# Weight blocks of a dequantised feed-forward layer: one row of scales and one of zero points each, a fourth staging slot, and another order on VectorE and GpSimd

## The reference, cut to what matters

```python
def dequant_gptq(qweight, scales, zeros, groupsize):       # groupsize 128
    q = qweight[k // PACK, :] >> (k % PACK * 4)[:, None] & 15
    z = zeros[:, n // PACK] >> (n % PACK * 4)[None, :] & 15
    zp = (z.astype(jnp.float32) + 1.0) * s
    return q.astype(jnp.float32) * s[g] - zp[g]            # g = k // groupsize
gate = x2 @ Wg                                             # Wg, Wu: 512 x 1376
up = x2 @ Wu
inter = gate * jax.nn.sigmoid(gate) * up
out = (inter @ Wd).astype(jnp.float16)                     # Wd: 1376 x 512
```

## Time and profile before

| | |
|---|---|
| median of 3 runs | 893.2 us (892.1 to 893.83) |
| profiled execution, device time | 893.42 us |
| its span in the trace | 891.5 us |
| VectorE busy | 715.8 us |
| TensorE busy | 701.6 us |
| GpSimd busy | 542.7 us |
| ScalarE busy | 420.6 us |
| DMA engines busy, mean | 32% |

### The profile page before, as it was taken

How to read it: one execution, slowest core, us unless ns; L and a number is a source line. 1 busy time by engine, 2 the same in 40 slices (tenths; PEclk the granted TensorE clock), 3 DMA queues, 4 the chain that set the end, 5 groups by cost and what they waited for, 6 DMA issues and landing times. The chain is left out here.

```text
span 891.5 us, 8190 instructions
## 1 busy us (share of the span) xinstructions
PE 701.6 (79%) x2700; PEld 316.2 (35%) x2700; DVE 715.8 (80%) x719; ACT 420.6 (47%) x699; POOL 542.7 (61%) x281
## 2 busy tenths in 40 slices
PE   6986669998766978346643499798999978999895
PEld 3322123332211322011110144343445534787774
DVE  4846999989999999999999896988464573676657
ACT  2344776687646764555544224333334343522331
POOL 0008899989989999899999555577002031341152
PEclk9998868999878999567775599899999989999998
DMA  9102423331425432673322067983300020000011
GB/s 277 45 26 102 149 76 100 119 118 56 180 97 183 148 117 84 183 207 118 118 89 77 18 144 193 251 200 79 142 0 1 1 96 0 1 1 1 1 47 48
DMA packets 65212, 86.72 MB, mean 97 GB/s; under 512 B 18308, under 2 KB 32407, under 8 KB 64914
## 3 DMA queue, kind: packets, MB, share of 16 engines
q1 hardware_dynamic: 65170, 86.20, 32.0%
HBM read 74.97 MB, written 11.21 MB: 97 GB/s over the span
## 5 line engine op out<-in xcount | busy, mean ns | idle before, releaser
L1965 POOL TENSOR_TENSOR dbu<-rep_du,bc 128x1024 f32<-128x1024 f32 x128 | 299.0, 2358 | 6.4 <-DVE psum L1066 3.7
L1645 ACT ACTIVATE psum<-rep_dt,aneg 128x512 f32<-128x512 f32 x256 | 166.1, 682 | 148.2 <-DVE hc L1077 118.9
L1066 DVE TENSOR_TENSOR_SCAN psum<-psum,dbu 128x1024 f32<-128x1024 f32 x87 | 198.7, 2284 | 7.7 <-ACT psum L1645 5.1
L845 PE MATMUL psum<-hc,stk 128*32 128x512 f32 x512 | 91.8, 798 | 75.9 <-POOL hc L1974 38.0
L1077 DVE TENSOR_TENSOR hc<-psum,bc 128x1024 f32<-128x1024 f32 x87 | 106.5, 1224 | 3.4 <-PE psum L845 0.4
L1974 POOL TENSOR_TENSOR hc<-hc,bc 128x1024 f32<-128x1024 f32 x41 | 96.5, 2354 | 11.6 <-DVE hc L1066 11.4
L1066 DVE TENSOR_TENSOR_SCAN hc<-psum,dbu 128x1024 f32<-128x1024 f32 x41 | 93.5, 2280 | 6.6 <-ACT psum L1645 4.2
L642 PE MATMUL psum<-xf_hi,gu_hi 128*128 128x512 f16 x176 | 67.7, 385 | 0.0
L642 PE MATMUL psum<-xf_hi,gu_lo 128*128 128x512 f16 x176 | 67.4, 383 | 0.0
L642 PE MATMUL psum<-xf_lo,gu_hi 128*128 128x512 f16 x176 | 67.2, 382 | 0.0
L642 PE MATMUL psum<-xT,w_g 128*128 128x512 f32 x120 | 59.4, 640 | 6.9 <-DVE dt_t L1085 6.9
(11 more groups left out here) (225 smaller groups left out, 1399.1 us busy)
## 6 DMA issues: line engine op xcount, KB each, us to landing
rep_dt<-rep_scratch SPq DMA_DIRECT2D x60, 256.0 KB, 3.3
rep_du<-rep_scratch SPq DMA_DIRECT2D x60, 256.0 KB, 4.3
q_gu<-qgu_in SPq DMA_DIRECT2D x11, 512.0 KB, 4.5
z_gu<-zgu_scratch SPq DMA_DIRECT2D x11, 512.0 KB, 6.6
bc<-bc_scratch SPq DMA_DIRECT2D x16, 256.0 KB, 4.3
rep_scratch<-du_t SPq DMA_DIRECT2D x15, 256.0 KB, 2.0
rep_scratch<-dt_t SPq DMA_DIRECT2D x15, 256.0 KB, 2.3
q_d<-qd_in SPq DMA_DIRECT2D x11, 256.0 KB, 5.0
```

What stands on the lines that cost most here:

```text
L845: last = pe.matmul(y_rows(k), stk[:], hc[:, (i + k // 2) % HCS, k % 2, :], start=False, stop=(s == GN - 1))
L1066: dve.tensor_tensor_scan(h, a, dbu[:, i % DBS].rearrange("p e t -> p (e t)"), 0.0, ALU.mult, ALU.add)\
L1645: last = act.activation(psum[:, 2 * (i % 2) + e, :], rep_dt[:, cc % 2, k, :], ACT.Exp, scale=aneg[:, k, c, n:n + 1])
L1965: pool.tensor_tensor(dbu[:, i % DBS], rep_du[:, cc % 2, k:k + 2, :], bc[:, n, :].unsqueeze(1).broadcast_to([P, 2, L]), ALU.mult).then_inc( ...
```

## The change

The zero points and the scales of a block are stored near the start as one row each (1536 numbers: gate and up, then down), by four transfers instead of two. `stage(i)` loads each row by one transfer (`scl` and `zp`), so it issues four transfers. A fourth slot is added. It lies where the product's input of b = 1 lay, so `stage(3)` now waits for the last tile of `out_part`, and the loads for attention move behind the last use of that slot. GpSimd starts on gate and up as soon as their scaling is done, and makes `d_lo` of block i-1 after the zero points of block i. ScalarE waits for gate and up and for down apart; its order stays the same, but for one small copy of a gate weight that moves from k = 8 to k = 11. VectorE unpacks three blocks ahead, after the low half of the block before it, instead of four blocks ahead and before that low half.

```diff
-        STG = [155, 43, 171]
+        STG = [155, 43, 171, 125]
@@ stage(i), SyncE
-                s = i % 3
+                s = i % SLOTS
                 load(q_gu[s][:], ...)
                 load(q_d[s][:], ...)
-                load(s_gu[s][:]..., sgu_in[:, cols]...broadcast_to([P, 2 * KH, P]), ld_stage[s])
-                load(z_gu[s][:]..., zgu_dram[:, cols]...broadcast_to([P, 2 * KH, P]), ld_stage[s])
-                load(s_d[s][:], sd_in[i:i + 1, :].broadcast_to([P, H]), ld_stage[s])
-                load(z_d[s][:], zd_dram[i:i + 1, :].broadcast_to([P, H]), ld_stage[s])
+                load(scl[s][:], s_dram[i:i + 1, :].broadcast_to([P, SZ]), ld_stage[s])
+                load(zp[s][:], z_dram[i:i + 1, :].broadcast_to([P, SZ]), ld_stage[s])
@@ SyncE, order of the loads
-            stage_again(3)
-            for i in range(4, 7):
+            wait_taken(sp_, ("out", 1, NT - 1))
+            stage(3)
+            for i in range(SLOTS, IC):
                 stage_again(i)
-            wait_taken(sp_, ("out", 1, NT - 1))
+            sp_.wait_ge(wlo_gu, 8)
+            sp_.wait_ge(wlo_d, 8)
             load(wqraw[:].rearrange("p a b c -> p (a b c)"), wq_in, ld_att)
...
-            for i in range(7, IC):
-                stage_again(i)
@@ VectorE, feed-forward of b = 0
             unpack(0)
-            for i in range(1, 4):
+            for i in range(1, 3):
                 unpack(i)
                 low_weights(i - 1)
             for i in range(IC):
                 ffn_inner(0, i)
...
-                if i + 4 < IC:
-                    unpack(i + 4)
+                if i + 2 < IC:
+                    low_weights(i + 2)
                 if i + 3 < IC:
-                    low_weights(i + 3)
+                    unpack(i + 3)
-                if i == 7:
+                if i == 9:
                     dve.wait_ge(ld_att, 16 * 7)
@@ high_weights(i), ScalarE
-                act.wait_ge(w_done, 2 * (i + 1))
-                act.copy(gu_hi[:, i, :], w_gu[i % 3][:]).then_inc(whi_done, 1)
-                act.copy(d_hi[:, i, :], w_d[i % 3][:]).then_inc(whi_done, 1)
+                act.wait_ge(w_done, 2 * i + 1)
+                act.copy(gu_hi[:, i, :], w_gu[i % SLOTS][:]).then_inc(whi_done, 1)
+                act.wait_ge(w_done, 2 * i + 2)
+                act.copy(d_hi[:, i, :], w_d[i % SLOTS][:]).then_inc(whi_done, 1)
@@ GpSimd
             for i in range(IC):
-                s = i % 3
+                s = i % SLOTS
+                pool.wait_ge(q_done, 2 * i + 1)
+                pool.tensor_tensor(w_gu[s][:], w_gu[s][:], z_gu[s], ALU.subtract).then_inc(w_done, 1)
                 pool.wait_ge(q_done, 2 * i + 2)
-                pool.tensor_tensor(w_gu[s][:], w_gu[s][:], z_gu[s][:], ALU.subtract).then_inc(w_done, 1)
-                pool.tensor_tensor(w_d[s][:], w_d[s][:], z_d[s][:], ALU.subtract).then_inc(w_done, 1)
-                pool.wait_ge(whi_done, 2 * i + 2)
-                pool.tensor_tensor(d_lo[:, i, :], w_d[s][:], d_hi[:, i, :], ALU.subtract).then_inc(wlo_d, 1)
+                pool.tensor_tensor(w_d[s][:], w_d[s][:], z_d[s], ALU.subtract).then_inc(w_done, 1)
+                if i:
+                    low_down(i - 1)
+            low_down(IC - 1)
```

More of the change, by code:

```diff
@@ L41 @@
 NPAIR = NCH * QP
+SZ = 2 * KH * P + H
+SLOTS = 4
 BIG = 1e30
@@ L248, in build @@
         d_lo = at("d_lo", 114, [IC, H], F16)
-        STG = [155, 43, 171]
+        STG = [155, 43, 171, 125]
         q_gu = [at(f"q_gu{s}", k, [2 * KH * P], I32) for s, k in enumerate(STG)]
         w_gu = [at(f"w_gu{s}", k, [2 * KH * P]) for s, k in enumerate(STG)]
-        s_gu = [at(f"s_gu{s}", k + 4, [2 * KH * P], F16) for s, k in enumerate(STG)]
-        z_gu = [at(f"z_gu{s}", k + 6, [2 * KH * P]) for s, k in enumerate(STG)]
-        q_d = [at(f"q_d{s}", k + 10, [H], I32) for s, k in enumerate(STG)]
-        w_d = [at(f"w_d{s}", k + 10, [H]) for s, k in enumerate(STG)]
-        s_d = [at(f"s_d{s}", k + 12, [H], F16) for s, k in enumerate(STG)]
-        z_d = [at(f"z_d{s}", k + 13, [H]) for s, k in enumerate(STG)]
+        q_d = [at(f"q_d{s}", k + 4, [H], I32) for s, k in enumerate(STG)]
+        w_d = [at(f"w_d{s}", k + 4, [H]) for s, k in enumerate(STG)]
+        zp = [at(f"zp{s}", k + 6, [SZ]) for s, k in enumerate(STG)]
+        scl = [at(f"scl{s}", k + 12, [SZ], F16) for s, k in enumerate(STG)]
+        z_gu = [t[:, 0:2 * KH * P] for t in zp]
+        z_d = [t[:, 2 * KH * P:] for t in zp]
+        s_gu = [t[:, 0:2 * KH * P] for t in scl]
+        s_d = [t[:, 2 * KH * P:] for t in scl]
         xf_hi = [at(f"xf_hi{b}", k, [KH, L], F16) for b, k in enumerate([187, 195])]
@@ L329, in build @@
         rep_stored = sem("rep_stored")
-        ld_stage = [sem(f"ld_stage{s}") for s in range(3)]
+        ld_stage = [sem(f"ld_stage{s}") for s in range(SLOTS)]
         ld_att = sem("ld_att")
@@ L1231, in unpack @@
                                        ALU.bitwise_and))
-                dve.tensor_tensor(w_gu[s][:], q_gu[s][:], s_gu[s][:], ALU.mult).then_inc(q_done, 1)
-                dve.tensor_tensor(w_d[s][:], q_d[s][:], s_d[s][:], ALU.mult).then_inc(q_done, 1)
+                dve.tensor_tensor(w_gu[s][:], q_gu[s][:], s_gu[s], ALU.mult).then_inc(q_done, 1)
+                dve.tensor_tensor(w_d[s][:], q_d[s][:], s_d[s], ALU.mult).then_inc(q_done, 1)
             def low_weights(i):
                 dve.wait_ge(whi_done, 2 * i + 1)
-                dve.tensor_tensor(gu_lo[:, i, :], w_gu[i % 3][:], gu_hi[:, i, :], ALU.subtract).then_inc(wlo_gu, 1)
+                dve.tensor_tensor(gu_lo[:, i, :], w_gu[i % SLOTS][:], gu_hi[:, i, :], ALU.subtract)\
+                    .then_inc(wlo_gu, 1)
             def low_turned(b):
@@ L1857, in _ @@
                     high_weights(k + 3)
[L1858 removed]
+                if k == IC:
                     act.wait_ge(ld_att, 16 * 7)
@@ L1996, in _, with low_down @@
                         pool.tensor_tensor(x[:, t, :], x[:, t, :], obuf[0][:, t, :], ALU.add).then_inc(out_done, 1)
+            def low_down(i):
+                pool.wait_ge(whi_done, 2 * i + 2)
+                pool.tensor_tensor(d_lo[:, i, :], w_d[i % SLOTS][:], d_hi[:, i, :], ALU.subtract).then_inc(wlo_d, 1)
             for i in range(IC):
[L2000 removed]
+                s = i % SLOTS
+                pool.wait_ge(q_done, 2 * i + 1)
+                pool.tensor_tensor(w_gu[s][:], w_gu[s][:], z_gu[s], ALU.subtract).then_inc(w_done, 1)
                 pool.wait_ge(q_done, 2 * i + 2)
[L2002 to L2005 removed]
+                pool.tensor_tensor(w_d[s][:], w_d[s][:], z_d[s], ALU.subtract).then_inc(w_done, 1)
+                if i:
+                    low_down(i - 1)
+            low_down(IC - 1)
             def low_moe_weights(n, names):
```

31 lines of the change are left out of this document (13 added, 18 removed).

## The result

| | before | changed |
|---|---|---|
| median | 893.5 us of 4 runs (892.1 to 894.36) | 922.17 us of 4 runs (914.78 to 926.11) |
| ratio, 95% interval | | 1.031 (1.025 to 1.038) |
| profiled execution | 893.42 us, span 891.5 | 922.13 us, span 920.3 |
| `it(0)` | 547.72 | 551.58 |
| `it(0)` to `it(10)` | 88.6 us | 111.0 us |

The changed kernel is slower. Its two busiest elementwise engines are busy for less time than before, so it is not work that was added but waiting. Where it stands is seen in VectorE's rows in time over one iteration of the changed kernel (start, length, line, output and inputs, and in brackets the idle time before and what ended it). They answer to the earlier trace rows.

What follows compares the result with a forecast made beforehand. VectorE was taken to bound each feed-forward block at 8.79 us; the change's 10.9 us ring would delay `it(8)` by 22.0 us and the end by 22.2, 893.4 + 22.2 = 915.6, stated as 915.5 us, range 910 to 921.

Steps and rivals of the forecast that it cites:

- The ring: Feed-forward layer of b = 0: VectorE, GpSimd and ScalarE form one chain from `it(k)` to `it(k+1)`, 10.9 us per iteration against 8.8.
- the transfers are worth 0: Loads of weight rows: four issues for six, same bytes, no engine waiting from 542.3 us on; 0 us, slot 3 bound 0 to 2.
- VectorE is released by `sg`: Sign before each `it` of blocks 3 to 8: VectorE idle over 4 us until ScalarE's silu output `sg` releases it.
- the rest of the span is the same work in the same order, so a shift at `it` of block 10 is a shift of the end: After the feed-forward stage of b = 0: no weights unpacked, so its shift of 22.2 us carries unchanged to the end.
- which TensorE sets and which stays: Start of the feed-forward stage: `it(0)` stays at 547.72 us because TensorE's output product sets it.
- range: Whole kernel: 910 to 921 us, leaving out B, C and the ends of A and D.
- GpSimd's order: GpSimd in the feed-forward stage: no longer waiting for ScalarE between its three instructions gains nothing by itself, 51.7 of 94.0 us busy.
- A: TensorE's clock falls after each gap; next to nothing within the ring, 2.9 us once after `it(8)`: 918.4 us; chance 0.21.
- B: Feed-forward stage: the ring does not bind, TensorE sets 7.9 us per block, total 879 us; chance 0.06.
- C: Feed-forward stage: no change, a ring of about 8.8 to 9 us, early gains paying for later loss; chance 0.03.
- D: Load of slot 3 and its followers late, `unpack(3)` waiting up to 5 us once: 917 to 921 us; chance 0.08.
- VectorE loses 2.7 us a block to GpSimd before the change: Feed-forward blocks: `it_lo`, `q_gu` and `w_d` run long waiting for the shared SBUF port, about 2.7 us per block.

Runs made afterwards that it cites:

- the kernel with the ring opened: Changed kernel with ScalarE making the high halves of block k+2 in iteration k instead of k+3; 900.58 us against 895.8, ratio 1.006, iteration 8.79 us.

## Why the prediction was wrong in its number and right in its mechanism

**The ring** (the main step) was right. Term by term, from the rows above of the changed kernel and the earlier trace rows:

| term | forecast | measured |
|---|---|---|
| `it` to behind `it_lo` | 2.05 | 610.85 - 608.81 = 2.04 |
| `gu_lo` | 1.14 | 611.99 - 610.85 = 1.14 |
| `q_gu`, `q_d`, `w_gu` | 2.33 | 614.30 - 611.99 = 2.31 |
| `w_d`, then GpSimd's two | 0.69 + 3.5 = 4.19 | 618.45 - 614.30 = 4.15 |
| `d_hi`, silu, handovers | 1.2 | 619.60 - 618.45 = 1.15 |
| sum | 10.9 | 10.79 |

In the fourth term the way differed and the size did not: GpSimd starts 0.17 us after `w_d` begins, and its `w_gu` is the longer for it (2.73 for 2.34), where the forecast let it stand idle for 0.69. Iterations 0, 1 and 2 took 15.6, 15.7 and 15.1 us (forecast 15.1, 15.7, 15.1), `it(0)` to `it(8)` 100.4 us (forecast 100.4; that it fits to the tenth is luck, 0.5 us too little in iteration 0, most of it the wait for slot 3, and 0.5 too much in the five of 10.9), and `it(0)` to `it(10)` 111.0 us (forecast 658.5 - 547.7 = 110.8). That the transfers are worth 0 was right (kernel with the rows alone, 1.000), but for 0.3 to 0.4 us of waiting for slot 3. That VectorE is released by `sg`, ScalarE by GpSimd, and that the three long instructions become short was right; TensorE's gap was 2.90 in the steady iteration.

**The step that failed** is "the rest of the span is the same work in the same order, so a shift at `it` of block 10 is a shift of the end", with `it(0)` "which TensorE sets and which stays". Two terms are missing from the sum through it, 3.9 us ahead of the stage and 2.5 behind it.

- *Ahead of the stage.* `it(0)` came at 551.58, 3.9 us later, for a reason that has nothing to do with the change: the scan layer ended 3.7 us later in that execution. In the second profile it ended at 509.1 and `it(0)` came at 547.95. The first execution of the kernel before, on which the sum was built, was a short one: of 61 runs in the later comparisons the medians were 895.0 to 895.8, not 893.2.
- *Behind the stage.* The second profile of the changed kernel (918.56 us) and the first of the kernel before (893.42) have scan layers of equal length, so their difference of 25.1 us is the change's. 22.4 of it lie between `it(0)` and `it(10)`, 0.2 ahead of them, and 2.5 behind them, where both kernels run the same instructions in the same order, but for ScalarE's one copy of a gate weight. The copy isn't the cause: the kernel with GpSimd's part alone does not move it, and from `it(10)` to VectorE's last instruction it takes 254.7 us, as the changed kernel does, where the kernel before takes 252.0 and 252.1 (2.7 us in these rows; what the device time has outside them is 0.2 less). VectorE's `it` of the last block of b = 1 comes at 740.99 before and 764.45 after (0.9 us of the 2.5); from the first `top` (the last layer's routing; 751.95 and 775.42) to VectorE's last instruction (888.3 and 913.62) it takes 136.4 and 138.2 us. Two windows of the same work, first before, then changed (busy times, granted clock, share and rate of transfers):

```profile
785.00:790.00 5.00, 5.00 (x26) 4.21 (x26) 4.02 (x4) 0.60 (x1) 0.82 (x1) 1.00 0.00 0
```

```profile
808.50:813.50 5.00, 5.00 (x20) 4.14 (x20) 3.89 (x4) 0.00 (x0) 0.00 (x0) 0.66 0.00 0
```

Both profiles of the changed kernel have this spell and both of the kernel before do not, so it goes with the kernel, as far as two profiles of each can tell. What in the shifted timing calls it forth was not found.

Forecast 915.6 on an execution of 893.4, plus 0.2 and 2.5 and 0.2 of rounding in the ring, gives about the 918.6 of the second profile; the first profile's 922.13 is above it by its scan layer, 3.6 us. The three executions beside it have no trace. Chance had a part in which side of 921 the median fell: the first four runs gave 922.17, the second four 917.8. The **range** failed with the same step: it took its width from the ring alone (10.4 to 11.3 us), where the ring was good to 1%, and gave none to the executions' own spread of some 12 us, nor to what stands behind the stage.

**GpSimd's order** "by itself gives nothing": wrong, as its own kernel showed (ratio 1.012). It was held to be no bound because 51.7 of 94.0 us were busy; but its last use of a slot sets when the slot is loaded again, and where its instructions stand sets whom VectorE meets.

**Rivals.** A, the clock: the mechanism exists, and within the ring it cost next to nothing, as forecast; but it did not show once after `it(8)`. There the stage ran on as before (10.65 us to `it(10)`, forecast 10.6), and the fall that cost time came 150 us later. That A's 918.4 lies beside the 918.56 of the second profile is luck. The windows of the changed kernel (columns as in the earlier trace rows) with the gap of iteration 2 and with the gaps of two of the steady ones:

```profile
595.00:600.00 5.00, 2.02 (x5) 0.74 (x6) 1.30 (x2) 3.34 (x5) 1.48 (x2) 0.77 0.43 111
...
615.00:620.00 5.00, 2.10 (x10) 0.79 (x9) 0.40 (x1) 2.16 (x3) 4.53 (x3) 1.00 0.36 146
...
640.00:645.00 5.00, 3.81 (x11) 1.40 (x12) 3.09 (x4) 1.73 (x3) 1.11 (x1) 0.71 0.01 2
```

and TensorE in time at the last of them and at `it(8)`:

```profile
641.20 0.39 PE L640 MATMUL psum<-xf_hi,gu_hi 128*128 128x512 f16 x1 [2.84 <-ACT sg L1813]
...
651.98 0.39 PE L640 MATMUL psum<-xf_hi,gu_hi 128*128 128x512 f16 x1 [1.16 <-ACT sg L1813]
```

In the first window the idle time before a matmul was 4.90 us and the clock fell; in the second it was 2.90 us, and the clock stayed at full speed there and in the next 5 us; in the third it was 2.84 us, and the clock fell all the same (0.50 from 642.5 to 645.0). The slow matmuls there only filled the next gap, 1.16 us for 2.84, and the iteration lasted 10.79 us as the others. The second profile has the same falls. The Trainium skill (TensorE: Matmul & The Clock Gate, on oscillation) tells of a loop whose clock falls anew behind every wait; here it fell behind all three gaps of 4.7 to 5.4 us and behind the last of the three of 2.8 to 2.9 us, not behind the other two. B (no binding ring) was wrong: in the changed kernel `sg` came late in every iteration up to `it(8)`. Its number was wrong too: the kernel with the ring opened stops at 8.79 us, and 7.89 was reached only with most of `d_lo` left out. C was wrong; it is what the order of before gives. D: the load of slot 3, issued at 546.9 us, was waited for once, 0.41 us, in iteration 0.

**VectorE loses 2.7 us a block to GpSimd before the change** was right as an observation and misleading as a price. The Trainium skill (SBUF — State Buffer, on the port pair) says that the pair is held for a whole instruction and that the second comer waits. The relay of the opened kernel agrees, and so does `w_d` with an input in PSUM, 0.68 us beside a running `d_lo` where it took 1.65. But taking one meeting away moves part of it to the next instruction: 0.97 us were taken from `w_d` and 0.60 came out of the iteration.

## What to carry to other kernels

Before an instruction is moved later on one engine, follow what it releases through the other engines until it comes back: here VectorE's unpacking, two engines on, released the very silu that VectorE waits for next, and a slack of one iteration became a ring of 10.8 us through three engines that were each idle for part of it. The length of the ring could be summed from the rows of before, start to start, to 1%; it was opened here by giving back one iteration of lead at ScalarE's link, and moving a step out of it gave next to nothing, because the step landed on something else that the ring needs. Take two profiles of a kernel before building on one execution's total, and give the range the spread of what lies outside the edited stage.
